# Flow attention in a two-layer graph network: VectorE adds up q and k, tiles prepared further ahead, two banks in the attention's output, clearing shared with ScalarE

## The reference

```python
q = sigmoid(heads(x @ Wq + bq)); k = sigmoid(heads(x @ Wk + bk)); v = heads(x @ Wv + bv)   # 8 heads of 64
sink_incoming   = 1 / einsum('nhld,nhd->nhl', q + EPS, k.sum(axis=2) + EPS)
source_outgoing = 1 / einsum('nhld,nhd->nhl', k + EPS, q.sum(axis=2) + EPS)
...                                      # conserved sums, softmax over the sources
kv = einsum('nhld,nhlm->nhdm', k, v * source_competition[..., None])
o  = einsum('nhld,nhdm->nhlm', q * sink_incoming[..., None], kv) * sink_allocation[..., None]
sa = o @ Wo + bo                          # then x + sa, a layer norm, gelu(h @ W1 + b1) @ W2 + b2
```

## Time and profile before

| | us |
|---|---|
| median of three runs | 1950.9 (1947.69 to 1954.26) |
| span of the profiled execution | 1942.5 |
| its own device time | not given; the median of the runs lies 8.4 above the span |
| `flow_attention`: last instruction ends (GpSimd) | 498.05 |
| next block's first load is issued | 505.66 |
| first and last scatter issue | 67.2 and 476.8 |
| granted TensorE clock, mean | 0.967 |

### The profile page before, as it was taken

How to read it: one execution, slowest core, us unless ns; L and a number is a source line. 1 busy time by engine, 2 the same in 40 slices (tenths; PEclk the granted TensorE clock), 3 DMA queues, 4 the chain that set the end, 5 groups by cost and what they waited for, 6 DMA issues and landing times. The chain is left out here.

```text
span 1942.5 us, 26152 instructions
## 1 busy us (share of the span) xinstructions
PE 1701.7 (88%) x8051; PEld 1109.0 (57%) x8052; DVE 891.8 (46%) x2244; ACT 542.0 (28%) x1504; POOL 747.3 (38%) x866
## 2 busy tenths in 40 slices
PE   4569988898588888898799997899999999999996
PEld 4134433545477777544344455677667767767773
DVE  6942267445699999788466666100000000000001
ACT  0011101122488888411111134122112112212212
POOL 0477777777788888740111101300000000052004
PEclk9999999999799999998799997899999999999998
DMA  7100083010200000102100044647205400420003
GB/s 219 30 2 2 2 312 110 9 29 13 79 1 0 1 0 0 53 3 104 49 1 0 1 173 154 198 178 300 83 16 194 189 19 19 189 75 16 22 23 105
DMA packets 75433, 144.18 MB, mean 74 GB/s; under 512 B 21017, under 2 KB 22633, under 8 KB 71149
## 3 DMA queue, kind: packets, MB, share of 16 engines
q1 hardware_dynamic: 48743, 118.60, 16.8%
q0 software_dynamic: 18976, 10.95, 2.5%
q10 hardware_dynamic: 7656, 13.97, 2.1%
HBM read 107.75 MB, written 35.69 MB: 74 GB/s over the span
## 5 line engine op out<-in xcount | busy, mean ns | idle before, releaser
L329 POOL DMA_INDIRECT sorted_edges<-fa_records,fa_edge_slot x313 | 310.2, 991 | 162.7 <-issue 100.4
L2044 PEld LDWEIGHTS et_ps_h<-ex_turned,arena 128*128 128x128 f32 x3072 | 348.9, 193 | 20.5 <-issue 20.5
L2044 PE MATMUL et_ps_h<-ex_turned,arena 128*128 128x128 f32 x3072 | 349.2, 276 | 9.3 <-issue 9.3
L2054 PE MATMUL et_ps_y<-arena,et_hidden_t 128*128 x768 | 337.5, 592 | 0.0
L1955 DVE TENSOR_SCALAR ex_turned<-et_ps_t,ex_ln_g,ex_ln_b 128x128 f32<-128x128 f32 x96 | 32.8, 403 | 583.5 <-PE et_ps_t L2024 583.5
L2054 PEld LDWEIGHTS et_ps_y<-arena,et_hidden_t 128*128 128x128 f32 x768 | 142.2, 190 | 160.7 <-issue 160.7
L1043 POOL TENSOR_SCALAR ad_row<-iota,ad_edges 128x128 fp32r<-128x128 f32 x295 | 209.7, 722 | 39.7 <-PE ad_ps L1119 29.8
L1096 ACT ACTIVATE ad_row_high<-ad_row,ad_edges 128x128 fp32r<-128x128 f32 x472 | 184.2, 391 | 48.4 <-DVE ad_row L1065 33.1
L1118 PE MATMUL ad_ps<-ad_to,ad_row_high 128*128 128x320 f32 x472 | 153.4, 337 | 49.1 <-ACT ad_row_high L1096 45.9
L1926 POOL DMA_INDIRECT xn_rows<-slot_out,from_slots x10 | 12.1, 1215 | 475.0 <-POOLq L1923 472.2
L1063 DVE TENSOR_SCALAR ad_to<-iota,ad_edges 128x320 fp32r<-128x320 f32 x472 | 167.7, 414 | 9.9 <-DMA ad_edges<-sorted_edges 9.9
(11 more groups left out here) (399 smaller groups left out, 2149.9 us busy)
## 6 DMA issues: line engine op xcount, KB each, us to landing
arena<-L_ffn_W SPq DMA_DIRECT2D x16, 4096.0 KB, 18.4
slot_rows<-fa_zeros SPq DMA_DIRECT2D x1, 7424.0 KB, 28.4
slot_out<-fa_zeros SPq DMA_DIRECT2D x1, 7168.0 KB, 50.5
slot_out<-et_y ACTq DMA_DIRECT2D x24, 256.0 KB, 2.0
et_rows_in<-slot_rows ACTq DMA_DIRECT2D x24, 256.0 KB, 2.7
sorted_edges<-fa_records,fa_edge_slot POOLq DMA_INDIRECT x313, 2.1
arena<-x SPq DMA_DIRECT2D x1, 2500.0 KB
neighbour<-fa_Wv SPq DMA_DIRECT2D x10, 250.0 KB
```

The lines of the kernel that those rows point to most:

```text
L329: nc.gpsimd.indirect_dma_start(g.sorted_edges, bass.IndirectOffsetOnAxis(ap=self.edge_slot[0:rows, e:e + 1], axis=0), self.records[0:rows, ...
L2044: last = pe.matmul(ps_h[:, f % 2, i, :], x.weights[:, at:at + P], turned[:, k, :], start=(k == 0), stop=(k == KD - 1))
L2054: last = pe.matmul(ps_y[:], hidden_t[:, i, :], x.weights[:, bass.ds(buffer * (2 * HALF) + (HALF + i * D), D)], start=(i == 0), stop=(i == ...
```

## The change

- TensorE no longer adds up q and k tile by tile. VectorE adds tile t to `q_sum` and `k_sum` (`add_to_sums`, 9 additions each), and TensorE multiplies each sum by the ones once, at the end. Two semaphores are new, `q_summed` and `k_summed`.
- VectorE prepares tile t + 2, instead of t + 1, ahead of tile t's biases, and in the feed-forward tile t + 3 instead of t + 2.
- `attend` uses `ps_b` and `ps_c` in turn and waits for `d_out` of tile t - 2.
- GpSimd's seven memsets go. ScalarE writes zeros to these parts (and w1, w2) with copies of up to 1024 columns: nine during the attention's output, seven during the feed-forward, two at the end. VectorE clears three of its four work buffers before the last `add_up` and the fourth at the end.

```diff
-            pool.wait_ge(s["d_out"], T + 1)
-            for part in (qkv[:, 0], qkv[:, 1, 2:], wo, mixed_w, kv_t, k_sum, q_sum):
-                nc.gpsimd.memset(part, 0.0).then_inc(s["cleared"], 1)
             for t in range(T):
...
+            def add_to_sums(t):
+                for name, of, total in (("q", q, q_sum), ("k", k, k_sum)):
+                    dve.wait_ge(s[name + "_ready"], t + 1)
+                    if t > 1:
+                        dve.wait_ge(s[name + "_summed"], t - 1)
+                    v.tensor_tensor(total[r, :], tile(of, 0) if t == 1 else total[r, :], tile(of, t),
+                                    ALU.add).then_inc(s[name + "_summed"], 1)
...
-            staggered(c, 4, prepare, add_biases, nothing)
+            prepare(0, 0)
+            prepare(1, 1)
+            for t in range(T):
+                if t + 2 < T:
+                    prepare(t + 2, t % 2)
+                if t >= 2:
+                    add_to_sums(t - 1)
+                add_bias("q", ps_a, q, t)
+                add_bias("k", ps_b, k, t)
+                if t == T - 1:
+                    add_to_sums(t)
+                add_bias("v", ps_c, v_, t)
...
-                c.link(v.tensor_tensor(work2[r, u, :], out(ps_b), rows["bo"][r, :], ALU.add))
+                c.link(v.tensor_tensor(work2[r, u, :], out((ps_b, ps_c)[u]), rows["bo"][r, :], ALU.add))
...
-            prepare_ff(0, 0)
-            prepare_ff(1, 1)
-            for t in range(T):
-                if t + 2 < T:
-                    prepare_ff(t + 2, t % 2)
+            for t in range(3):
+                prepare_ff(t, t % 2)
+            for t in range(T):
+                if t + 3 < T:
+                    prepare_ff(t + 3, (t + 1) % 2)
+                if t == T - 1:
+                    dve.wait_ge(s["f_turned"], T + 2)
+                    c.settle()
+                    c.step(v.memset(arena[:, 3 * T * D:3 * T * D + 3 * D], 0.0))
                 add_up(t, t % 2)
             c.settle()
-            c.link(v.memset(arena[:, 3 * T * D:3 * T * D + 4 * D], 0.0))
+            c.link(v.memset(work2[:, 1, :], 0.0))
...
+            def clear(part):
+                n = part.shape[1] // D
+                nc.scalar.copy(part.rearrange("p (n d) -> p n d", n=n),
+                               positions.zeros[:].unsqueeze(1).broadcast_to([P, n, D])).then_inc(s["act_cleared"], 1)
...
+            behind_mix = [arena[:, at:at + 2 * D] for at in range(T * D + 2 * D, 2 * T * D, 2 * D)]
+            behind_mix += [wo.rearrange("p k d -> p (k d)")[:, i * 2 * D:(i + 1) * 2 * D] for i in range(2)]
+            behind_mix += [kv_t.rearrange("p k n -> p (k n)"), k_sum, q_sum]
+            behind_attend = [arena[:, at:at + 2 * D] for at in range(0, T * D, 2 * D)]
+            behind_attend += [mixed_w.rearrange("p k d -> p (k d)")[:, i * 2 * D:(i + 1) * 2 * D] for i in range(2)]
...
+                if t < len(behind_mix):
+                    clear(behind_mix[t])
...
+                if t == 0:
+                    act.wait_ge(s["d_done"], T + 2)
+                if t < len(behind_attend):
+                    clear(behind_attend[t])
+            clear(w1.rearrange("p k n -> p (k n)"))
             act.wait_ge(s["f_done"], T + 2)
...
+            clear(w2.rearrange("p k n -> p (k n)"))
...
-            staggered(b, 0, turn(s["in_ready"], s["turned_out"], work), project, add_sums)
+            turn_in = turn(s["in_ready"], s["turned_out"], work)
+            turn_in(0, 0)
+            for t in range(T):
+                if t + 1 < T:
+                    turn_in(t + 1, (t + 1) % 2)
+                project(t, t % 2)
+            pe.wait_ge(s["q_summed"], T - 1)
+            pe.matmul(ps_q, ones, q_sum[0:NT, :], start=True, stop=True)
+            pe.wait_ge(s["k_summed"], T - 1)
+            pe.matmul(ps_k, ones, k_sum[0:NT, :], start=True, stop=True).then_inc(s["sums_done"], 1)
...
             def attend(t, u):
                 pe.wait_ge(s["d_ready"], t + 1)
-                pe.wait_ge(s["d_out"], t + 1)
-                linear(ps_b, u, mixed_w).then_inc(s["d_done"], 1)
+                if t >= 2:
+                    pe.wait_ge(s["d_out"], t)
+                linear((ps_b, ps_c)[u], u, mixed_w).then_inc(s["d_done"], 1)
```

23 lines of the change are left out of this document (6 added, 17 removed).

## The result

| | us |
|---|---|
| median before, 4 runs beside the changed kernel | 1950.07 (1947.69 to 1954.26) |
| median after, 4 runs | 1937.49 (1934.51 to 1939.74) |
| ratio after to before | 0.9929, 95% interval 0.9913 to 0.9946 |
| profiled execution after: own time, span | 1939.74, 1937.9 |
| forecast | 1941.0, range 1936.5 to 1946.5 |

The ratio is 13.9 us of 1950.07, with its interval 10.5 to 17.0; the forecast was 9.9. In a second set, with 24 runs of the kernel before, the pair gave 1945.01 and 1935.22: ratio 0.9946 (0.9923 to 0.9969), 10.5 us, with its interval 6.0 to 15.0. The forecast gain lies just outside the first interval and inside the second.

What follows compares the result with a forecast made beforehand. GpSimd's scatter and the memsets behind it were taken to set the block's end, with VectorE right behind. Memsets gone, 12.94 us, less 3 us of longer scatter issues, gave 1950.9 - 9.9 = 1941.0 us, range 1936.5 to 1946.5.

Steps and rivals of the forecast that it cites:

- The changed kernel ends with GpSimd's tail, and the compute's gain is hidden: Flow-attention block's end: TensorE's part ends some 43 us earlier, mostly hidden behind GpSimd's scatter; only GpSimd's tail counts.
- projections: Projection stage: sums off TensorE and tiles prepared earlier, so it ends 27.8 us sooner.
- attention's output: Attention's output stage: two banks in turn remove the waits for one bank, 6 us less.
- feed-forward: Feed-forward stage: preparing three tiles ahead removes TensorE's waits, 9 to 10 us less, 9.5 in the sum.
- The terms on GpSimd: GpSimd's tail at the block's end: 12.94 us of memsets gone, less 3 us of longer scatter issues, 9.9 us gained.
- the holds: GpSimd's scatter: issues lengthened by VectorE operations with two SBUF inputs, growing by 3 us, bounds nothing to 10.4.
- Seven memsets gone: Behind GpSimd's last scatter: the seven large memsets vanish, 12.94 us, their parts cleared by ScalarE during earlier stages.
- rival (a): GpSimd's scatter: the sums hold no issue, or the phase is luckier; 12.94 us less, 1938.0 us; chance 0.23.
- Block end: End of the flow-attention block: 498.05 less 12.94 gives 485.1 us, before 3 us of longer scatter issues.
- the base: Whole kernel: 8.4 us between the profiled span 1942.5 and median 1950.9, taken as time around the span.
- The second step that failed: Block's end: shortening the compute alone gives nothing, GpSimd alone 0.34 us, since VectorE ends right behind it.
- VectorE's 0.34 us as the price of clearing alone: Block's end: with only GpSimd shortened, VectorE's last memset at 497.71 leaves a gain of 0.34 us.

Runs made afterwards that it cites:

- e2: Changed kernel with GpSimd's seven memsets put back and ScalarE's sixteen early clears removed, so the compute's half alone: 1946.31 us, ratio 1.001 to the kernel before.
- e6: Changed kernel with 36 more VectorE additions, both inputs in SBUF, in the projections: 1936.0 us, ratio 0.9958 to the kernel before.
- e1: The kernel before, run and profiled once more with no edit: 1945.98 us, ratio 1.0003.
- sets A: The first two measuring sets, in which the kernel before took 1945.0 and 1945.2 us; only kernels of one kind of set are compared.
- e3: Kernel before with only the clearing of GpSimd's seven memset parts moved to ScalarE: 1940.23 us, ratio 0.9973.
- e5: Changed kernel with the sums of q and k back on TensorE, tile by tile: 1933.68 us, ratio 0.995 to the kernel before.
- e11: Kernel before with GpSimd's seven memsets cut into 29 pieces of 512 columns: 1943.59 us, ratio 0.9999.
- sets B: Three later measuring sets on three chips, in which the kernel before took 2274.7, 2275.1 and 2275.0 us.
- e4: Changed kernel with the twelve memsets behind GpSimd's scatter moved to VectorE: 1929.7 us, ratio 0.9913 to the kernel before.
- e18: Changed kernel with GpSimd's twelve last memsets on VectorE and the sums on TensorE, measured in sets B: 2243.34 us, ratio 0.9855 to the kernel before there.

## Where the prediction was right, and where it was wrong

- **The changed kernel ends with GpSimd's tail, and the compute's gain is hidden: right.** The compute got 44.3 us shorter (43.3 forecast) and is worth nothing by itself (e2). Its parts: projections 27.5 (27.8 forecast), attention's output 6.8 (the last L707 at 391.4, 34.3 before L691 at 425.7; 6 forecast), feed-forward 10.0 (9.5 forecast).
- **The terms on GpSimd: right in sum, the holds partly by luck.** Seven memsets gone, 12.94. The holds were 3.4 us by the busy sum in the first trace, 1.1 in the second, 3.0 for the mean (3 forecast, and rival (a) had none). Block end forecast at 488.1, measured 489.2 and 486.7; load forecast near 496, measured 496.8 and 494.3. The sum for the holds had 1.5 to 2.2 us in the projections and 0.6 in the feed-forward. In the first trace after, measured against the kernel before, they grew by 0.4 and 1.8, and by 1.0 in the two stages between; in the second by 0.4, 1.1 and -0.3. So the size of the sum came out and its parts didn't. Rival (a)'s 0.93 us for each of 57 issues divides a time cut off at the window's edges by issues counted whole; their median was 0.958 us and the longest 1.07. e6 and the count of held issues show that VectorE operations with two inputs in SBUF cause the holds, so here the row was the better guide than the inference that the Trainium skill (SBUF — State Buffer, Who interferes with whom) makes for descriptor generation.
- **The first step that failed, the base: "its own device time isn't given, the median of three is 1950.9, 8.4 us more, which I take as what lies around the span".** The runs with both numbers have 1.7 to 2.0 us between time and span (single ones up to 2.3). So the profiled execution had a time of 1942.5 + 1.9 = 1944.4, some 6 us under the median of its three runs and close to the medians of 49 later ones (1945.0 and 1945.2). With the measured 1.9 in place of 8.4 the sum gives 1944.4 - 9.9 = 1934.5, against 1937.49 and 1935.22 measured; 1941.0 was 3.5 and 5.8 us above them. My sum took its gain from one execution and its base from others, which were longer.
- **The second step that failed: "Shortening the compute alone would give nothing, because GpSimd ends last; shortening GpSimd alone would give 0.34 us, because VectorE is right behind it", read from one execution as the state of the kernel before.** The compute and GpSimd lie side by side there. In that execution GpSimd never waited; in e1 it waited 4.99 us for the feed-forward and the block ended 5.8 us later. TensorE's end came 8.0 us later, 4.4 by its granted clock in three products and 3.6 by the memset that held VectorE (2.70 us for 0.54) and the clock behind that; GpSimd's tail covered 2.2 of the 8.0. The changed kernel is free of both, since its compute ends 31 us before the last scatter. So the gain at the block's end has a term that the sum lacks: 0 in one execution, 5.8 in the other. How often it comes isn't shown. By the load, the four pairs of executions before and after gain 8.8 to 17.1 us, 13.0 on average; by the span only 4.6 to 14.4, 9.5 on average. That this term is what lies between 9.9 and the 13.9 us of the first set is therefore argued and not shown; the 10.5 us of the second need no such term.
- **VectorE's 0.34 us as the price of clearing alone** was wrong as well (4.0 us by the trace, 1.75 of them from an earlier compute): the 7.6 us behind the block are GpSimd's, 7.17 of them its DRAIN, and I had read them as a meeting that follows whichever engine is last.
- **Open.** From the next block's first load to the end of the span it takes 1433.0 to 1441.6 us in sets A, in kernels with the same code there. The five executions with the sums on TensorE (before, e1, e3, e5, e11) have 1433.0 to 1436.8, the five with the sums on VectorE 1438.8 to 1441.6. In sets B the two groups overlap (1438.4 to 1443.0 and 1437.8 to 1445.3). So whether the change costs some us behind the block, or single traces differ by as much, is open; no experiment was made on it. Also open are what GpSimd's DRAIN does and the cause of sets B.

## What to carry to other kernels

Where two engines end a block within a microsecond of each other, take the end apart in at least two executions: which of them is last can change with the granted clock, the gain of a change that frees both can be larger than the sum read from one, and each half alone shows little. Before you cost an edit at the end of a block, ask which engine the meeting really follows, by comparing kernels in which the order of the ends differs and by looking at the sequencers' own instructions there; here only GpSimd's counted, and the last microseconds came from moving its memsets to an idle engine (e4, 0.9913). Subtract a span from the same execution's time before you add a sum to a median.

## What the runs showed of the hardware that I had not expected

- Behind a block in which GpSimd had memsets last, 7.61 to 7.62 us pass until the next block's first load, in twelve executions of eight kernels; VectorE worked until 5.7 us before that load without moving it. 7.17 us of it are GpSimd's DRAIN, which the busy time doesn't count; with 253 scatters in place of 313 it is 2.27. Where GpSimd was through long before, the load came 0.49 us behind VectorE (e18).
- A GpSimd memset of 5120 columns (4.36 us) held a VectorE `tensor_scalar` of 512 columns, so that it took 2.70 us instead of 0.54. The other way round, a VectorE memset of 5120 columns held no scatter issue (e4). VectorE operations with two inputs in SBUF held 412 of 1374 issues, mostly up to 1.50 us, 0.08 us for each further addition; operations with at most one held none of 830.
- The same program's compute ended 8.0 us later in one execution than in another; three products under a granted clock of 0.50 to 0.68 made 4.4 us of it.
- In three of five sets all engines but GpSimd moved in steps of some 22 us while it scattered, and the kernel before took 2275 us instead of 1945, on a chip that had run it in 1945 us. There a change to the compute counts in full that is hidden elsewhere.
